# Spectra of all rows from high and low parts, and a second table of chain steps, in a decoder kernel on one core

## The reference, cut to what matters

```python
# autocorrelation, per row b and head: Q from x, K = V = context
qf = jnp.fft.fft(q, axis=2)
kf = jnp.fft.fft(k, axis=2)
corr = jnp.fft.ifft(qf * jnp.conj(kf), axis=2).real
w, idx = jax.lax.top_k(corr.transpose(0, 1, 3, 2), topk)      # topk = 9
w = jax.nn.softmax(w, axis=-1)
for i in range(topk):
    g = jnp.minimum(idx[:, :, None, :, i] + pos, L - 1)
    out = out + w[:, :, None, :, i] * jnp.take_along_axis(v, g, axis=2)
# Sinkhorn, per token on a 4x4 matrix, 50 times
u = -jax.nn.logsumexp(Z + v[..., None, :], axis=-1)
v = -jax.nn.logsumexp(Z + u[..., :, None], axis=-2)
```

## Time and profile before

| | |
|---|---|
| median of 3 runs | 1224.99 us (1220.55 to 1226.48) |
| the profiled execution | 1223.23 us |
| its span in the trace | 1221.4 us |
| granted TensorE clock over the span | 0.931 |
| TensorE busy | 1028.0 us (84%) |
| VectorE busy | 921.5 us (75%) |
| ScalarE busy | 596.9 us (49%) |
| GpSimd busy | 442.5 us (36%) |

### The profile page before, as it was taken

How to read it: one execution, slowest core, us unless ns; L and a number is a source line. 1 busy time by engine, 2 the same in 40 slices (tenths; PEclk the granted TensorE clock), 3 DMA queues, 4 the chain that set the end, 5 groups by cost and what they waited for, 6 DMA issues and landing times. The chain is left out here.

```text
span 1221.4 us, 23230 instructions
## 1 busy us (share of the span) xinstructions
PE 1028.0 (84%) x7866; PEld 759.1 (62%) x7866; DVE 921.5 (75%) x2819; ACT 596.9 (49%) x1789; POOL 442.5 (36%) x619
## 2 busy tenths in 40 slices
PE   5889999999999999999657999999999897615056
PEld 4667777777777787777445677776555554313034
DVE  6756787666787666786614878778999999996994
ACT  6534545544555544455515667766564564212023
POOL 0613443333443333443313766663433343110020
PEclk9989999999999999999778999999999998857579
DMA  9011011111011111011132222422222211148025
GB/s 380 29 59 42 17 58 58 58 58 41 22 53 58 58 58 41 29 48 42 45 102 86 87 91 74 130 91 74 89 92 97 77 54 39 44 135 326 0 52 138
DMA packets 47234, 95.71 MB, mean 78 GB/s; under 512 B 5952, under 2 KB 30400, under 8 KB 47168
## 3 DMA queue, kind: packets, MB, share of 16 engines
q1 hardware_dynamic: 47168, 94.91, 23.1%
HBM read 64.48 MB, written 27.26 MB: 75 GB/s over the span
## 5 line engine op out<-in xcount | busy, mean ns | idle before, releaser
L628 POOL TENSOR_TENSOR prob_G<-prob_G,rl 128x512 f32<-128x512 f32 x96 | 99.8, 1041 | 250.4 <-DVE rl L513 250.4
L390 ACT ACTIVATE prob_G<-prob_G,negm 128x128 f32<-128x128 f32 x384 | 148.8, 388 | 83.9 <-DVE negm L455 83.9
L245 PE MATMUL ps_qkv<-w_hi,xT_hi 128*128 128x512 f32 x384 | 156.3, 407 | 17.4 <-DVE prob_G L518 9.2
L246 PE MATMUL ps_qkv<-w_lo,xT_hi 128*128 128x512 f32 x384 | 151.0, 393 | 0.0
L247 PE MATMUL ps_qkv<-w_hi,xT_lo 128*128 128x512 f32 x384 | 150.8, 393 | 0.0
L319 PE MATMUL ps_qkv<-wo_hi,aT_hi 128*128 128x512 f32 x256 | 108.5, 424 | 0.0
L321 PE MATMUL ps_qkv<-wo_hi,aT_lo 128*128 128x512 f32 x256 | 102.6, 401 | 0.0
L320 PE MATMUL ps_qkv<-wo_lo,aT_hi 128*128 128x512 f32 x256 | 102.4, 400 | 0.0
L245 PEld LDWEIGHTS ps_qkv<-w_hi,xT_hi 128*128 128x128 f32 x384 | 72.7, 189 | 44.6 <-issue 21.8
L451 DVE TENSOR_TENSOR prob_G<-ps_s,mask 128x512 f32<-128x512 f32 x96 | 64.9, 676 | 44.4 <-PE ps_s L228 43.9
L480 DVE TENSOR_TENSOR xT_lo<-ps_t,xT_hi 128x512 fp32r<-128x512 f32 x16 | 11.1, 692 | 100.2 <-ACT xT_hi L418 100.2
(11 more groups left out here) (252 smaller groups left out, 2658.2 us busy)
## 6 DMA issues: line engine op xcount, KB each, us to landing
xin<-in_x SPq DMA_DIRECT2D x16, 512.0 KB, 3.3
xres<-in_x SPq DMA_DIRECT2D x16, 512.0 KB, 5.5
x<-xres SPq DMA_DIRECT2D x16, 512.0 KB, 2.6
c_xin<-x SPq DMA_DIRECT2D x16, 512.0 KB, 4.3
c_b_xres<-x SPq DMA_DIRECT2D x16, 512.0 KB, 3.2
rows_x<-c_row SPq DMA_DIRECT2D x64, 128.0 KB, 2.3
m_xm<-rows_x SPq DMA_DIRECT2D x16, 512.0 KB, 8.7
out<-m_ot SPq DMA_DIRECT2D x64, 128.0 KB, 2.4
```

Source lines behind the costliest of these rows:

```text
L245: nc.tensor.matmul(ps_qkv[:, n, :], xT_hi[:, k, :], w_hi[:, k, cols], start=k == 0, stop=False)
L246: nc.tensor.matmul(ps_qkv[:, n, :], xT_hi[:, k, :], w_lo[:, k, cols], start=False, stop=False)
L390: r = nc.scalar.activation(prob(g)[:, j, :], prob(g)[:, j, :], ACT.Exp, bias=negm[:, h:h + 1], accum_out=lsum[:, h:h + 1])
L628: nc.gpsimd.tensor_tensor(prob(g), prob(g), rl[:, g * GROUP:(g + 1) * GROUP].rearrange("p (j o) -> p j o", o=1).to_broadcast([P, GROUP, T] ...
```

## The change

**What it does to the spectra.** `whole`, `c_whole` and all branches on them are gone, so rows 9 to 15 are made as rows 0 to 8 are: ScalarE copies the high parts, GpSimd subtracts for the low parts, and TensorE makes each half from three products. The context of these rows comes into `cin`.

```diff
-        c_whole, c_lo = [], []
-        for i in range(2):
-            with ExitStack() as shared:
-                c_whole.append(shared.enter_context(nc.sbuf_tensor(f"c_c_whole{i}", [P, D], F32)))
-            c_lo.append(sb(f"c_lo{i}", [P, D], F32R))
+        c_lo = [sb(f"c_lo{i}", [P, D], F32R) for i in range(2)]
...
-        def whole(n):
-
-            return isinstance(n, int) and n >= 9
...
-                if ahead and whole(b + 2):
-                    sp.wait_ge(v_ps, 2 * (b + 1))
-                    sp.dma_start(c_whole[par][:], ctx_in[b + 2]).then_inc(cin_in, 16)
-                elif ahead:
+                if ahead:
                     sp.wait_ge(chi_done, b + 2)
                     sp.wait_ge(clo_done, b + 2)
                     sp.dma_start(cin[:], ctx_in[b + 2]).then_inc(cin_in, 16)
...
-                    if lo is None:
-                        r = nc.tensor.matmul(dst[:, n, :], mats[:, i, :], hi[:, cols], start=True, stop=True)
-                        continue
...
-                    split3(p_a, 0, *((xn, None) if whole(c) else (xn_hi, xn_lo))).then_inc(q_ps, 1)
+                    split3(p_a, 0, xn_hi, xn_lo).then_inc(q_ps, 1)
...
-                if whole(n):
-                    act.wait_ge(q_ps, n)
-                    act.wait_ge(xnl_done, 9)
-                elif later(n, 0):
+                if later(n, 0):
                     act.wait_ge(xnl_done, n)
...
             def split_normalised(n):
-                if whole(n):
-                    return
                 pool.wait_ge(xnh_done, n + 1)
```

**The table of steps.** The new file has two definitions of `autocorrelation_phase` in one module. The first is the old function's head with the new table of steps, and behind the table a copy of the engine programs of `attention_phase`. Then `Chain` and its helpers stand once more, and the second definition, which is complete and holds the old table. The added lines, cut to the two tables:

```diff
         for b in range(8, B - 1):
+            if b == 13:
+                parts = {0: at + 2, 1: at + 6, 2: END[0], 3: END[1], 4: END[1] + 12}
+            else:
+                parts = {0: at + 2, 1: at + 6, 2: at + 20, 4: at + 28}
...
+def autocorrelation_phase(nc, x1, ctx_in, ident, dft, w24, base, wb, norm2, facts, chains, rows_x, rows_y):
...
             if b == 11:
                 parts = {0: at + 3, 1: at + 9, 2: END[0], 3: END[1], 4: END[1] + 10}
             else:
                 parts = {0: at + 3, 1: at + 9, 2: at + 29, 4: at + 40}
```

More of the change, by code:

```diff
@@ new lines, in autocorrelation_phase @@
+        W = T // NS
+        ROW_DMAS = 16 * (NS + 1)
+        one_a, one_b, one_c = chains
+        END = (BASES[1] - 2, BASES[1], BASES[2] - 2, BASES[2])
+        steps_to = {(6, 0): ((one_a, 2),), (6, 2): ((one_a, 3),), (6, 4): ((one_a, 6),),
+                    (7, 1): ((one_a, 7),), (7, 2): ((one_a, 8),)}
+        at = 8
+        for b in range(8, B - 1):
+            if b == 13:
+                parts = {0: at + 2, 1: at + 6, 2: END[0], 3: END[1], 4: END[1] + 12}
+            else:
+                parts = {0: at + 2, 1: at + 6, 2: at + 20, 4: at + 28}
+            for part, to in parts.items():
+                steps_to[b, part] = ((one_a, to),)
+            at = parts[4]
@@ new lines, in iterations @@
+        def iterations(engine, body):
+            body(-2, attend=False, project=False, norm=True)
+            body(-1, attend=False, project=True, norm=True)
+            body(0, attend=True, project=True, norm=True, first=True)
+            with engine.Fori(1, B - 3) as b:
+                body(b, attend=True, project=True, norm=True)
+            body(B - 3, attend=True, project=True, norm=True)
+            body(B - 2, attend=True, project=True, norm=False)
+            body(B - 1, attend=True, project=False, norm=False)
@@ new lines, in advance @@
+def advance(dve, chain, to, most=1000):
+    for k in range(chain.issued + 1, min(to, chain.issued + most) + 1):
+        if k > 1:
+            dve.wait_ge(chain.step, k - 1)
+        if k in (3, 4, 7, 8):
+            dve.wait_ge(chain.logs, {3: 1, 4: 2, 7: 3, 8: 4}[k])
+        for n in range(len(BLOCK_ITERS)):
+            if k == BASES[n] + 2:
+                dve.wait_ge(chain.logs, FIRST_LOGS + n * BLOCK_LOGS)
+            if k == BASES[n + 1] - 1:
+                dve.wait_ge(chain.logs, FIRST_LOGS + n * BLOCK_LOGS + 2)
+        sinkhorn_step(chain, k).then_inc(chain.step, 1)
+        chain.issued = k
@@ new lines, in weave, with sb, sem @@
+def weave(dve, *targets):
+    while any(chain.issued < to for chain, to in targets):
+        for chain, to in targets:
+            advance(dve, chain, to, 1)
+def autocorrelation_phase(nc, x1, ctx_in, ident, dft, w24, base, wb, norm2, facts, chains, rows_x, rows_y):
+    with ExitStack() as ctx:
+        def sb(name, shape, dt=F32):
+            return ctx.enter_context(nc.sbuf_tensor("c_" + name, shape, dt))
+        def sem(name):
+            return ctx.enter_context(nc.semaphore("c_" + name))
+        idf = sb("b_idf", [P, P])
+        mats = sb("mats", [P, N_DFT, P])
+        fwd_hi = sb("fwd_hi", [P, 4, P], F32R)
+        fwd_lo = sb("fwd_lo", [P, 4, P], F32R)
+        w24_sb = sb("w24_sb", [P, KD, NLOG])
+        base_sb = sb("base_sb", [P, NLOG])
+        wb_sb = sb("wb_sb", [P, 2, C])
+        xin = sb("xin", [P, D])
+        xn = sb("xn", [P, D])
+        xn_hi = sb("xn_hi", [P, D], F32R)
+        xn_lo = sb("xn_lo", [P, D], F32R)
+        xres = sb("b_xres", [P, D])
+        cin = sb("cin", [P, D])
+        c_hi = [sb(f"c_hi{i}", [P, D], F32R) for i in range(2)]
+        c_lo = [sb(f"c_lo{i}", [P, D], F32R) for i in range(2)]
@@ L1049, in transpose_weights @@
                     r.then_inc(wT_ps, 1)
[L1051 removed]
                 if near:
[L1053 to L1057, removed]
+                    pe.wait_ge(xnh_done, c + 1)
+                    pe.wait_ge(xnl_done, c + 1)
                     if not far:
```

604 lines of the change are left out of this document (588 added, 16 removed).

## The result

The changed kernel took 1227.99 us in the median of 20 runs (1226.08 to 1234.06). The kernel before took 1224.82 us in 20 runs beside them (1220.21 to 1227.03). The ratio is 1.0037, with a 95% interval of 1.0025 to 1.0049: 3.1 to 6.0 us slower, 4.5 in the middle. That is a small loss, still within the 0.5% that the prediction called no change. The profiled execution of the changed kernel has a span of 1224.8 us; the one before had 1221.4.

The account below looks back on a forecast made before the run. VectorE's own instruction list was taken to set bodies 9 to 14. Terms -0.7 (body 8), +0.2 (ScalarE) and +4.4 (products held by GpSimd) made +3.9, 1228.9 us; own range 1225 to 1232, 8 in 10 1221 to 1238.

Parts of the forecast that it names:

- The table has no effect: Chain steps: the later definition, with the old table, is what runs, so the moved steps cost and bring nothing.
- Body 8 gains 0.7 us from TensorE: Body 8: TensorE's shorter halves bring the key spectra earlier; -0.7 us, bounds 0 and -1.0.
- The meeting at 838: Body 7's `xn_lo` meets VectorE's product and choices at 838, so ScalarE's squares come about 0.4 us later.
- ScalarE's push, +0.2: Bodies 7 and 8: two added copies per row push later ScalarE work; +0.2 us, bounds 0 and +0.6.
- The lock, +4.4 in bodies 8 to 13: VectorE products with both inputs in SBUF wait for GpSimd's current instruction to end; 18 meetings, +4.4 us.
- the walk: Bodies 8 to 13 with GpSimd's new bursts laid in, counting held products; +4.4 us, 3.0 to 5.5 if `c_lo` shifts.
- TensorE's saving is never on the path in bodies 9 to 14, and VectorE still waits for nothing: Bodies 9 to 14: TensorE waits for VectorE's residual, never the reverse, so its saved 1.6 us per row brings nothing.
- The lock's dear rival: Late bodies: 24 meetings lose 0.41 us each, 9.8 us; total +9.3, 1234.3 us; chance 22%.
- GpSimd not held in return: GpSimd's bursts: no term for VectorE delaying them, though by rule they might grow 0.1 to 0.2 us per meeting.
- TensorE's gain: Rival: TensorE sets the late bodies, so seven rows save 1.6 us each, 11 us; 1214 us; chance 4%.
- Missed meetings: Rival: GpSimd's bursts miss VectorE's products; -0.5, 1224.5 us; chance 8%.
- If the new table ran: net near 0: Rival: 84 steps leave the late bodies (-21 us) and return beside chain b; net near 0; chance under 1%.

Follow-up runs that it names:

- e1: Changed kernel, but GpSimd makes only 8 of 1024 columns of each low part of rows 9 to 15; 1223.23 us, ratio 0.9987.
- e5: Kernel before, with three fp32r products per half in rows 9 to 15 from older rows' tiles, no added copies or splitting; 1224.35 us, ratio 1.0010.
- e6: Changed kernel plus ten unused TensorE products between the q spectrum and first key spectrum of rows 9 to 15; 1228.61 us, ratio 1.0042.
- e2: Changed kernel, but rows 9 to 15 take each half as one f32 product of the high part, splitting kept; 1227.13 us, ratio 1.0020.
- after_again: The changed kernel's instructions once more, from a file without the first definition; 1227.88 us, ratio 1.0042 to the kernel before.
- e4: Kernel before, with the new table of steps in the function that runs and f32 spectra in rows 9 to 15; 1218.03 us, ratio 0.9945.
- e8: Kernel before, with GpSimd's scaling of the weights in four instructions of 128x256 from body 7 on; 1225.17 us, ratio 1.0014.

## Why the prediction was right, and where not

The forecast was 1228.9 us, +3.9; measured is 1227.99, +4.5 by the ratio. The direction, the size and the main cause are right. That the size came out so near is in part luck, as two errors of opposite sign are in it. Point by point:

- *The table has no effect.* Right: the kernel without its file's first definition gives the same lengths to 0.06 us.
- *Body 8 gains 0.7 us from TensorE.* Right in kind, small in size: e1 and e5 gain 0.92 and 0.93 (within the bounds of 0 and -1.0). In the changed kernel the wait fell by 1.45 us, but VectorE was also held there by 0.89 at 838 and 0.54 later, and the body is 0.27 us shorter where -0.7 + 0.2 + 0.68 = +0.18 was forecast. These three make -0.02, so 0.25 us of body 8 have no account. The meeting at 838 was named, with 0.4 us.
- *ScalarE's push, +0.2.* Not seen; e1 with the copies and e5 without them agree to 0.1 us.
- *The lock, +4.4 in bodies 8 to 13.* The mechanism is right and the size nearly: 3.35 us by the chain products that the walk counts, 4.24 with the one at 838. For the same products e6, where no spectrum is late, gives 4.36, and e2 2.71. The walk depends on phases, and e2 shows that its bounds of 3.0 to 5.5 are narrow below. The walk put `c_lo` of body 10 at 902.27, 12.30 us behind that body's mark; it came 13.52 us behind it (904.89 - 891.37), since the key spectrum was late and ScalarE's copy stands behind it; without late spectra (e6) it is 12.21.
- *TensorE's saving is never on the path in bodies 9 to 14, and VectorE still waits for nothing.* This step failed. It took "TensorE waits for VectorE's residual" as a reason that a faster TensorE costs nothing. The longer wait (2.00 and 1.33 us) let the granted clock fall to 0.55, the second key spectrum came late, and VectorE waited 1.89 us in three bodies; e6 puts the net cost at 1.75 us. The sum was short by about that, which the smaller lock in bodies 9 to 13 (2.78 in place of the walk's 3.69) and the end of the kernel partly gave back, so the total came out near the forecast with two terms off. The marks of bodies 9 and 10 lie 1.60 and 1.33 us further apart and that of body 14 0.02, where 0.4 to 1.1 was given. The prediction named waits in bodies 9 to 14 as a sign of its being wrong, and they are there.
- *The lock's dear rival* (24 meetings of 0.41 us, 9.8): not at this size of instruction. Its `xn_lo` does reach the choices, but with the old table of steps only the first one of body 8, and that in after_again, e2 and e6 (0.81 to 0.82 us), not in the profiled execution of the changed kernel. That was named as a sign of being wrong, and it costs 0.5 us once.
- *GpSimd not held in return.* The prediction reads the earlier trace rows as 2.79 and 2.80 us "with three such meetings and with none". By the earlier trace rows the burst of 2.80 meets one held product (908.88) and that of 2.79 two (910.30 and 911.45). That no term was made of it stays right, as the bursts in the changed kernel show.
- *TensorE's gain*: e5 gave 0.9 of 11 us. *Missed meetings*: no, held rose in each of bodies 8 to 13.
- *If the new table ran: net near 0.* Wrong. e4 gives -0.55%. The sum took the moved steps at their own length, but in the rows beside another chain's steps they cost 0.05 us each.

What stays open: what sets the phase of the clock in the mixing phase, how much the moved steps of e4 really cost, and why e5 and e1 differ in the whole time though their marks agree.

## What to carry to other kernels

When an engine that waits gets less work, ask what its longer idle time does to its clock, not only whom it waits for: here 11 us less work of TensorE gave 0.9 us, and cost 1.75 once the lock had lengthened its waits too. When work is added to GpSimd beside small VectorE products with both inputs in SBUF, count the meetings and the length of one GpSimd instruction, and not only GpSimd's busy time; and before work is cut into quarters, look for who waits for its end. Two independent chains of small dependent VectorE instructions are worth laying beside each other where both exist: a step of the shorter one added 0.05 us there in place of its 0.30.

## What the hardware showed that was not expected

- TensorE's clock fell to a granted 0.55 behind two idle times of 2.00 and 1.33 us with one half between them, and didn't behind 1.34 and 1.33 (e1) or 0.81 and 1.33 (e6). In body 13 it fell behind a wait of 2.60 us and didn't behind 2.32 (e1), while in body 10 it fell behind a wait of 1.63 us.
- A VectorE product of 0.24 us that met a GpSimd instruction of 2.36 us took 2.13, and ended 0.11 us behind it; one that met an instruction of 0.69 us took 0.64. The GpSimd bursts didn't grow by it in a way that can be seen: `c_lo` of body 10 took 2.81 us with such a meeting, and all four bursts there 2.79 to 2.83.
- The lock also holds a choice of the weights, which has two inputs in SBUF: 0.81 us in place of 0.34 (e2, e6).
- Four GpSimd instructions of 128x256 took 2.79 to 2.83 us where one of 128x1024 took 2.36, and for the weights 2.35 against 1.90; the small instructions right behind the four took 0.45 in place of 0.19 (e8).
- A dependent VectorE step of 128x20 to 128x80 has a start-to-start time of 0.30 us alone (the kernel before), and adds 0.05 us when it stands between the steps of another chain (e4).
